# Expert network: the rows of the first five tiles picked by products with 0/1 tables instead of being read back after the scatter

## The reference, cut to what matters

```python
def _L2_ffn_ref(x, gate_w, gate_b, w1, b1, w2, b2):
    probs = jax.nn.softmax(xt @ gate_w + gate_b, axis=-1)      # 8 experts
    _, idx = jax.lax.top_k(probs, 2)
    mask = (one_hot(idx).sum(axis=1) > 0)
    h1 = relu(einsum('th,ehf->etf', xt, w1) + b1[:, None, :])  # 128 -> 512
    out_e = einsum('etf,efh->eth', h1, w2) + b2[:, None, :]    # 512 -> 128
    return einsum('eth,te->th', out_e, mask)
x = x + _L2_ffn_ref(_layernorm(x), ...)
```

## Time and profile before

| | |
|---|---|
| median of three runs | 2870.22 us |
| the profiled execution | 2874.72 us |
| its span, first to last instruction | 2873.1 us |
| mean granted TensorE clock | 0.936 of full speed |
| TensorE busy | 2364.0 us (82%) |
| VectorE busy | 1789.9 us (62%) |
| ScalarE busy | 1395.5 us (49%) |
| GpSimd busy | 865.6 us (30%) |

### The profile page before, as it was taken

One profiled execution on the slowest core, in us unless ns is written; L12 is line 12 of the kernel. 1 busy time (PEld: TensorE's weight loads), 2 busy tenths in 40 slices (PEclk: granted clock), 3 DMA queues, 4 the chain that ended last, 5 costly groups with the idle time before them and its releaser, 6 DMA issues. The chain is left out here.

```text
span 2873.1 us, 37709 instructions
## 1 busy us (share of the span) xinstructions
PE 2364.0 (82%) x12952; PEld 1117.6 (39%) x12992; DVE 1789.9 (62%) x3191; ACT 1395.5 (49%) x2324; POOL 865.6 (30%) x858
## 2 busy tenths in 40 slices
PE   6678879999887889777866788799998877887777
PEld 2231244544355246223222313445443652562232
DVE  5958575555545725985659585755456456259865
ACT  5534636555433434645455356366554325346454
POOL 2822141000235333651038221510002353327410
PEclk8997999999988889999989989999999888899999
DMA  3002000000032131000000020000000321310000
GB/s 144 0 6 79 13 1 9 1 1 1 1 104 65 57 100 36 0 1 1 5 12 0 13 71 13 1 9 1 1 1 1 105 64 56 103 33 0 1 2 15
DMA packets 59110, 81.00 MB, mean 28 GB/s; under 512 B 10976, under 2 KB 39136, under 8 KB 58656
## 3 DMA queue, kind: packets, MB, share of 16 engines
q1 hardware_dynamic: 49568, 63.81, 6.9%
q0 software_dynamic: 4992, 10.76, 1.1%
q10 hardware_dynamic: 4352, 3.94, 0.5%
HBM read 53.83 MB, written 26.08 MB: 28 GB/s over the span
## 5 line engine op out<-in xcount | busy, mean ns | idle before, releaser
L2305 ACT ACTIVATE L1b_pr<-ps,L1b_mneg 128x512 f32<-128x512 f32 x256 | 173.5, 683 | 191.3 <-DVE L1b_mneg L2346 191.3
L2344 DVE TENSOR_REDUCE L1b_m<-ps 128x2 f32<-128x1024 f32 x128 | 156.7, 1224 | 88.7 <-PE ps L2195 83.6
L97 ACT ACT_TABLE_LOAD x44 | 56.5, 1283 | 262.4 <-PEq L503 58.7
L1540 POOL TENSOR_TENSOR L0a_db<-L0a_du,L0a_bs 128x1024 f32<-128x1024 f32 x64 | 150.4, 2359 | 106.6 <-DVE L0a_du L1654 60.0
L1540 POOL TENSOR_TENSOR L3a_db<-L3a_du,L3a_bs 128x1024 f32<-128x1024 f32 x64 | 150.3, 2358 | 98.5 <-DVE L3a_du L1654 59.0
L1979 ACT ACTIVATE L0b_pt<-ps 128x1024 f32<-128x1024 f32 x128 | 125.6, 1022 | 97.9 <-PE ps L1875 97.7
L2067 DVE TENSOR_REDUCE L0b_mx<-ps 128x1 f32<-128x512 f32 x256 | 157.9, 682 | 20.9 <-PE ps L1862 18.3
L274 POOL CAST L1g_xc<-xn 128x512 bf16<-128x512 f32 x2 | 1.5, 732 | 558.3 <-DVE xn L149 558.3
L2370 DVE COPY L1b_prt<-ps 128x512 f32<-128x512 f32 x128 | 88.5, 691 | 126.4 <-PE ps L2208 126.1
L1681 DVE TENSOR_TENSOR_SCAN L0a_hs<-ps,L0a_db 128x1024 f32<-128x1024 f32 x64 | 146.0, 2282 | 5.5 <-ACT ps L1460 5.5
L1681 DVE TENSOR_TENSOR_SCAN L3a_hs<-ps,L3a_db 128x1024 f32<-128x1024 f32 x64 | 146.0, 2281 | 3.4 <-ACT ps L1460 3.4
(11 more groups left out here) (701 smaller groups left out, 5367.1 us busy)
## 6 DMA issues: line engine op xcount, KB each, us to landing
L2f_wall<-expert_dram SPq DMA_DIRECT2D x32, 256.0 KB, 5.6
L2g_wall<-expert_dram SPq DMA_DIRECT2D x32, 256.0 KB, 5.3
weights<-w_dram SPq DMA_DIRECT2D x5, 941.5 KB, 13.8
L0b_qs<-stack_dram SPq DMA_DIRECT2D x32, 96.0 KB, 2.2
stack_dram<-L0b_cut SPq DMA_DIRECT2D x24, 128.0 KB, 2.1
L2b_qs<-stack_dram SPq DMA_DIRECT2D x32, 96.0 KB, 2.2
stack_dram<-L2b_cut SPq DMA_DIRECT2D x24, 128.0 KB, 2.1
L2f_xg<-slots SPq DMA_DIRECT2D x10, 288.0 KB, 4.5
```

What stands on the lines that cost most here:

```text
L1540: pool.tensor_tensor(db[:, n % DEEP, :, :], du[:, b, :, :], bcast(bs[:, n % DEEP, :], 1, 2), ALU.mult).then_inc(input_ready, 1)
L2305: act.activation(pr[:, s % 2, h, :], g.ps[:, 2 * (s % 2) + h, :], ACT.Exp, bias=mneg[:, s % 2, h:h + 1], accum_out=total[:, u % 2, t, h:h ...
L2344: dve.tensor_reduce(m[:, s % 2, :], g.ps[:, 2 * (s % 2):2 * (s % 2) + 2, :], AX.X, ALU.max).then_inc(max_raw, 1)
```

## The change

The rows of tiles 0 to 4 are no longer taken from `slots`. For each of these tiles VectorE builds a 0/1 table `where` (8 x 128 columns: for each block of 128 tokens, which token has which lane of the tile), from `lane`, which is 1 to 128 for a token that has a slot in the tile and 0 otherwise. TensorE then multiplies the token rows `tok` with the table (8 products that add up in PSUM), which gives the transposed tile directly. Tiles 5 to 22 are still read from `slots`, in groups of 1, 2, 4, 4, 4, 3; the row numbers of the first five tiles (columns 128 to 143) are read in one more DMA. All 16 scatters remain. The 70 idle products are taken out, the products of L543 and L544 write to PSUM banks 6 and 7, and their copies on ScalarE move into the loop over the first tiles.

```diff
-    GROUPS = (1, 2, 4, 4, 4, 4, 4)
+    AHEAD = 5
+    GROUPS = (1,) * AHEAD + (1, 2, 4, 4, 4, 3)
...
                 sp.wait_ge(sent, 16 * 2 * NT)
-                for k in range(groups):
+                for k in range(AHEAD, groups):
                     ...
+                    if k == AHEAD:
+                        sp.dma_start(xg[:, 0:AHEAD, P:WIDE], g.slots[0:AHEAD * P, P:WIDE].rearrange("(t p) w -> p t w", p=P)).then_inc(ids_in, 16)
...
+                pe.wait_ge(tok_in, 2 * NB)
...
-                pe.wait_ge(mask_in, NB)
-                idle_products(g, pe, 7, 70)
+                def gather(k):
+                    pe.wait_ge(where_ready, k + 1)
+                    if k >= 2:
+                        pe.wait_ge(x_in, k - 1)
+                    for t in range(NT):
+                        mm = pe.matmul(g.ps[:, 4 + k % 2, 0:P], tok[:, 0, t, 0:P], where[:, k % 2, t, :], start=(t == 0), stop=(t == NT - 1))
+                    mm.then_inc(x_turned, 1)
...
-                turn(0)
+                gather(0)
+                gather(1)
                 hidden_products(0)
-                for n in range(SLOTS):
+                for n in range(AHEAD - 1):
+                    if n + 2 < AHEAD:
+                        gather(n + 2)
+                    hidden_products(n + 1)
+                    results(n)
+                results(AHEAD - 1)
+                turn(AHEAD)
+                hidden_products(AHEAD)
+                for n in range(AHEAD, SLOTS):
...
                 choose(0)
+                x_copy(0)
                 choose(1)
-                x_copy(0)
-                for n in range(SLOTS):
+                x_copy(1)
+                for n in range(AHEAD):
+                    if n + 2 < AHEAD:
+                        x_copy(n + 2)
+                    choose(n + 2)
+                    if 1 <= n <= NB:
+                        take_mask(n - 1)
+                x_copy(AHEAD)
...
+                dve.tensor_tensor(away[:, :, :], bcast(slot_f[:, :], 1, AHEAD), bcast(g.w("e2_step", 0, AHEAD), 2, 2 * NT), ALU.subtract).then_inc(lane_step, 1)
...
+                def place_tokens(k):
+                    if k == 0:
+                        dve.wait_ge(lanes_ready, 1)
+                    if k >= 2:
+                        dve.wait_ge(x_turned, k - 1)
+                    dve.tensor_tensor(where[:, k % 2, :, :], bcast(lane[:, k, :], 2, P), bcast(g.w("e2_lane"), 1, NT), ALU.is_equal).then_inc(where_ready, 1)
...
+                place_tokens(2)
+                relus(0)
+                for n in range(AHEAD - 1):
+                    if n + 3 < AHEAD:
+                        place_tokens(n + 3)
+                    relus(n + 1)
+                    take_result(n)
+                take_result(AHEAD - 1)
                 rows_of(0)
-                relus(0)
+                rows_of(AHEAD)
+                relus(AHEAD)
...
-                    pool.wait_ge(rows_ready, group_of[n] + 1)
+                    pool.wait_ge(rows_ready, 1 if n < AHEAD else group_of[n] - AHEAD + 2)
```

More of the change, by code:

```diff
@@ L477, in expert_ffn @@
         xg = st.sb("xg", [P, SLOTS, WIDE])
+        away = st.sb("away", [P, AHEAD, 2 * NT])
+        lane = st.sb("lane", [P, AHEAD, NT])
+        where = st.sb("where", [P, 2, NT, P])
         xt = st.sb("xt", [P, 2, max(GROUPS), P])
@@ L586, in _ @@
                 pe.wait_ge(b2_in, 1)
+                pe.wait_ge(mask_in, NB)
                 for c in range(NT // 2):
@@ L606, in _, with take_mask @@
                 act.activation(b2_t[:, :], g.ps[0:E, 3, 0:P], ACT.Copy).then_inc(b2_in, 1)
-                for b in range(NB):
+                def take_mask(b):
                     act.wait_ge(mask_turned, b + 1)
-                    act.activation(mask_t[:, b * KT:(b + 1) * KT, :], g.ps[0:E, 4 + b, :].rearrange("e (t c) -> e t c", c=P), ACT.Copy).then_inc(mask_in, 1)
+                    act.activation(mask_t[:, b * KT:(b + 1) * KT, :], g.ps[0:E, 6 + b, :].rearrange("e (t c) -> e t c", c=P), ACT.Copy).then_inc(mask_in, 1)
                 def x_copy(k):
@@ L685, in _ @@
+                place_tokens(0)
+                place_tokens(1)
                 dve.tensor_tensor(start[:, :, :], tile_no, bcast(base[:, :], 1, SLOTS), ALU.is_ge).then_inc(plan, 1)
[L686 to L689, removed]
+                dve.scalar_tensor_tensor(out=limit[:, :], in0=base[:, :], scalar=float(P), in1=count[:, :], op0=ALU.mult, op1=ALU.add).then_inc(plan, 1)
@@ L690, in _ @@
+                dve.wait_ge(plan, 4)
                 dve.tensor_tensor(start[:, :, :], start[:, :, :], past[:, :, :], ALU.subtract).then_inc(plan, 1)
-                dve.scalar_tensor_tensor(out=limit[:, :], in0=base[:, :], scalar=float(P), in1=count[:, :], op0=ALU.mult, op1=ALU.add).then_inc(plan, 1)
                 dve.wait_ge(plan, 5)
@@ L719, in relus, with take_result @@
                     ins.then_inc(relu, 1)
+                def take_result(n):
+                    dve.wait_ge(out_ready, n + 1)
+                    dve.tensor_copy(y[:, n, :], g.ps[:, 2 + n % 2, 0:P]).then_inc(y_in, 1)
+                place_tokens(2)
[6 more added lines that the diff above has]
+                take_result(AHEAD - 1)
                 rows_of(0)
-                relus(0)
-                for n in range(SLOTS):
+                rows_of(AHEAD)
+                relus(AHEAD)
+                for n in range(AHEAD, SLOTS):
                     if n + 1 == first_of[group_of[n] + 1] and group_of[n] + 1 < groups:
@@ L2972, in _pack @@
     put("e2_id", (np.arange(2)[None, :, None] + 2 * (r[:, None, None] + 128 * np.arange(8)[None, None, :])).reshape(128, 16).astype(f))
+    put("e2_lane", over(np.arange(1, 129, dtype=f)))
     put("e2_tile", over(np.arange(SLOTS, dtype=f)))
```

34 lines of the change are left out of this document (24 added, 10 removed).

## The result

The changed kernel takes 2856.7 us (median of 7 runs, 2853.3 to 2864.8), the old one beside it 2871.6: ratio 0.9941 (0.9927 to 0.9955). That is 15 us less where 40 were forecast. The profiled execution took 2863.8 us (span 2862.2), 7 us above the median, so the passes shown here may have lost somewhat more than most.

What follows compares the result with a forecast made beforehand. The scatter chain, then tiles at 2.01 us each, were taken to set a pass's end. Terms -10.1 - 1.5 + 1.0 + 0.5 gave -10.1 us a pass, -40.4 over four: 2830 us, 8-in-10 range 2815 to 2850.

Steps and rivals of the forecast that it cites:

- this work is hidden with 2.6 us to spare: TensorE's work on the five early tiles ends at 839.0, before tile 5's rows land for 841.59.
- The sign that I had named for being wrong: First transposed row from `slots` over 2 us late, or TensorE getting there last.
- Tiles taken out: 18 tiles instead of 23 left behind the scatters, 5 x 2.01 = 10.1 us less a pass.
- Tables: VectorE builds each table in 1.225 us, in time for TensorE and hidden behind its 3.56 us a tile; cost 0.
- The 0.6 us for waits on relu and weights: Allowance added to TensorE's 17.8 us of products for the five early tiles, moving their end from 838.4 to 839.0.
- Scatters beside tables: GpSimd's sixteen scatters held up by VectorE's two-input tables: +0.5 us a pass, bounds 0 and 6.8.
- Clock at the restart: TensorE's shorter gap before tile 5 may keep 2.4 GHz: -1.5 us a pass, bounds 0 and -3.1.
- Extra DMA: Read of row numbers delays the group of tiles 6 and 7: stall 0.4 to 3.1 us, taken as +1.0.
- Results of five tiles waiting for the row numbers: GpSimd's waiting results catch up, a scatter each 1.26 us against a tile each 2.01 us: 0.
- Rival A: GpSimd's scatters held up by the tables, tile 5 up to 6.8 us later: 2859, by half 2846; chance 0.12.
- B: Extra DMA at its long end and TensorE's clock fallen at the restart: -7 us a pass, 2842; chance 0.09.
- C: TensorE falls to 1.2 GHz through waits for tables in the early tiles: +5 us a pass, 2890; chance 0.04.

## Why the prediction was wrong

The step that failed is "this work is hidden with 2.6 us to spare", with its end at 839.0. The products were costed rightly (3.56 us a tile; 3.58 with the scatters away). What I left out is that behind the second scatter TensorE had, in the old trace, done nothing for which another engine waited: the earlier trace rows shows 15.06 us of idle products whose end nobody awaited, so their records could not show late completions. In the changed kernel the work ended at 848.36, as links of its chain waited for signals that were up to 8 us late, and the first read row came 6.0 us late, 29.45 us behind the first scatter instead of 23.42 (5.6 over the passes): 1.8 for the scatters, 4.2 for TensorE. The sign that I had named for being wrong, a first row over 2 us late or TensorE last, held in both halves.

- Tiles taken out, -10.1: right; 9.6 less with the scatters away, ids DMA and restart at half clock included.
- Tables: 1.22 us each, tokens and weights in time: right. The 0.6 us for waits on relu and weights was the term that was wrong: 17.8 us of products took 27.3 us.
- Scatters beside tables, +0.5: +1.8 to +2.1 in the four passes, four times the forecast but within its bounds. The five tables held a scatter by 0.1 to 0.7 us each. The first sentence of the Trainium skill (SBUF — State Buffer, Who interferes with whom) is nearer here than its inference: a scatter takes up to 1.64 us beside a two-input table, 0.95 to 1.07 beside one-input instructions. It was never held for the table's whole 1.22 us.
- Clock at the restart, -1.5: the first read tile's groups took 1.13 us, near the best case, but not because the gap was short: TensorE was late and had none. First read row to first result's end is 4.93 us instead of 7.74: -2.8. That this made up for part of the loss was luck.
- Extra DMA, +1.0: 0, as TensorE came later than the rows. With the scatters away from the tiles, where TensorE waited for the rows, 9.6 of the 10.1 us were gained, which leaves some 0.5 for it. No run shows what a 64-byte piece costs.
- Results of five tiles waiting for the row numbers: costed at 0, as GpSimd "catches up". It does, and beside its scatters back to back TensorE's signals are late again: +2.7 from the first read tile's result to the end (36.93 us for 17 tiles of 2.01).
- Sum of the first pass: -10.1 + 6.0 - 2.8 + 2.7 = -4.2. By the trace it is 4.1: 75.43 us from the first scatter to the last result before (818.17 to 893.60), 71.31 after (818.75 to 890.06).

Rival A was right in its mechanism and a quarter of its size. B did not happen. C had a part of it right for another cause: TensorE did fall to 1.2 GHz within the five tiles, but behind late signals and not behind tables, for some 1.9 of the 4.2 us. None of them was "TensorE gets there last for want of a signal".

## What to carry to other kernels

Before putting chained work beside a burst of indirect DMAs, look whether the old trace shows any engine waiting for that engine during such a burst; idle products whose end nobody awaits prove nothing. Count products as well as time there: a few large ones get through better than many small ones. Where they must overlap, pauses of 0.94 us every four scatters took 2.2 us off a pass here, and pauses of 0.51 us did as well as those in the kernel with six tiles. Pacing the backlog helped with six tiles ahead (2.9 us a pass); alone, with five, it did not show.

## What the runs showed of the hardware

- Beside scatters issued each 1.26 us, TensorE's completions came at 1.6 wide and about 1.7 narrow products a us once it had run ahead (issued narrow ones: 14.5 a us without scatters). In step with ScalarE, nothing was late at 1.1 products a us, and at 3.2 a us nothing for six rounds of the first pass, then 1.2 and 3.4 us. Freely issued at 4.6 a us, products were reported up to 10.0 us late. At a slot scatter each 2.2 us no signal was late.
- TensorE kept issuing some 30 products ahead of its reports, so its records look undisturbed while its signals are late: by 6.4 us in the changed kernel's fourth table, by 11.6 us in the kernel with one-input tables (830.22 to 841.82). TensorE itself had no "remote" wait for VectorE or ScalarE in any expert pass of any run.
- The kernel with two-input VectorE instructions, which hold GpSimd's scatters up, was faster than the one with one-input instructions, which leave them alone (0.9941 against 1.0094 of the old kernel).
- What the scatters and TensorE's completions share was not found, nor whether it is GpSimd's issuing or the scatters' own DMA writes that matters. It stays open, as does why the lateness varies between passes of one kernel.
